# Spreading half 1's codes with TensorE and letting the loads go in steps, in a recommender tower on one core

## The reference

```python
e = jnp.stack([tbl_0[ids[:, 0]], ..., tbl_15[ids[:, 15]]], axis=1)        # 2048 x 16 x 16
A = jnp.repeat(x0, s, axis=1)                                             # x0: 2048 x 39 x 16
Bm = jnp.repeat(e, f, axis=2).reshape(b, s * f, d)
z = jnp.einsum('bnh,bnd,nk,khd,kd->bkh', A, Bm, alpha, w, hv[..., 0])      # 2048 x 16 x 16
h = jnp.concatenate([z.reshape(2048, -1), dense_ctx], axis=1)
h = jnp.maximum(h @ W_top1 + b_top1, 0.0)                                 # 272 -> 512
h = jnp.maximum(h @ W_top2 + b_top2, 0.0)                                 # 512 -> 256
y = h @ W_top3                                                            # 256 -> 1
```

## Time and profile before

| | |
|---|---|
| three runs | 177.66, 178.49 and 180.9 us, median 178.49 |
| the profiled execution | 178.92 us |
| its span, first to last instruction | 177.0 us |
| busy: PE, DVE, POOL, ACT | 164.0, 142.5, 110.9, 66.0 us |
| mean granted TensorE clock | 0.99 |

### The profile page before, as it was taken

How to read it: one execution, slowest core, us unless ns; L and a number is a source line. 1 busy time by engine, 2 the same in 40 slices (tenths; PEclk the granted TensorE clock), 3 DMA queues, 4 the chain that set the end, 5 groups by cost and what they waited for, 6 DMA issues and landing times.

```text
span 177.0 us, 5041 instructions
## 1 busy us (share of the span) xinstructions
PE 164.0 (93%) x2131; PEld 124.3 (70%) x2131; DVE 142.5 (80%) x177; ACT 66.0 (37%) x176; POOL 110.9 (63%) x116
## 2 busy tenths in 40 slices
PE   6549898968997999999999999999999999999993
PEld 1338696736984879696969696969686967776671
DVE  2978797893799999999899979996999899495000
ACT  3440788084881125212431243123403341451141
POOL 2777777777747777777777777777777776000000
PEclk9999999996999999999999999999999999999999
DMA  5889999999999997989498948694559360000000
GB/s 87 307 120 327 246 275 161 270 373 264 283 334 250 345 320 150 363 248 230 79 352 240 216 160 300 189 230 104 183 219 222 48 231 6 2 4 0 0 4 0
DMA packets 15085, 34.26 MB, mean 194 GB/s; under 512 B 6618, under 2 KB 10582, under 8 KB 11990
## 3 DMA queue, kind: packets, MB, share of 16 engines
q1 hardware_dynamic: 10162, 31.51, 58.9%
q0 software_dynamic: 3584, 0.92, 6.6%
q10 hardware_dynamic: 1316, 1.50, 2.9%
HBM read 33.88 MB, written 0.04 MB: 192 GB/s over the span
## 4 chain that ended last, share of the span: by engine, by line
PE 69%; DMA 13%; DVE 4%; ACT 3%; SPq 3%; issue 3%; POOL 3%; DVEq 0%
PE bank L927 17%; PE bank L842 17%; PE bank L848 15%; PE bank L894 11%; DMA ids_half_dram<-ids_half 6%; PE bank L915 5%; PE bank L835 4%; DMA ids_b<-ids_half_dram 3%; POOL e L478 3%; DMA e<-tbl_dram,ids_all 3%; DVE prod L642 2%; SPq L446 2%; DMA ids_all<-ids_dram 1%; ACT apart L724 1%; PE bank L856 1%
## 5 line engine op out<-in xcount | busy, mean ns | idle before, releaser
L478 POOL DMA_INDIRECT e<-tbl_dram,ids_all x112 | 110.7, 988 | 38.7 <-issue 33.2
L642 DVE TENSOR_TENSOR prod<-x,bank 128x2048 f32<-128x2048 f32 x40 | 90.3, 2279 | 8.8 <-issue 4.6
L927 PE MATMUL bank<-prod,m_w 128*32 128x256 f32 x640 | 38.6, 382 | 2.5 <-DVE prod L642 2.5
L894 PE MATMUL bank<-table,onehot 125*128 125x64 bf16 (+1 forms) x288 | 31.9, 198 | 2.3 <-DVE low L537 2.3
L842 PE MATMUL bank<-tower,w_z 128*128 128x256 f32 x128 | 32.8, 403 | 0.7 <-ACT tower L743 0.7
L894 PE MATMUL bank<-low,onehot 125*128 125x64 bf16 (+1 forms) x288 | 31.8, 197 | 0.0
L894 PE MATMUL bank<-rest,onehot 125*128 125x64 bf16 (+1 forms) x288 | 31.8, 199 | 0.0
L894 PEld LDWEIGHTS bank<-table,onehot 125*128 125x128 bf16 x288 | 27.4, 98 | 5.7 <-issue 2.9
L927 PEld LDWEIGHTS bank<-prod,m_w 128*32 128x32 f32 x640 | 19.1, 109 | 17.0 <-issue 3.5
L848 PE MATMUL bank<-tower,w 128*128 128x256 f32 x128 | 30.7, 382 | 0.1
L842 PEld LDWEIGHTS bank<-tower,w_z 128*128 128x128 f32 x128 | 24.2, 199 | 6.3 <-ACT tower L743 3.1
(11 more groups left out here) (60 smaller groups left out, 85.4 us busy)
## 6 DMA issues: line engine op xcount, KB each, us to landing
x<-x_dram SPq DMA_DIRECT2D x16, 1024.0 KB, 8.1
x<-x_dram SPq DMA_DIRECT2D x16, 512.0 KB, 12.4
ids_b<-ids_half_dram SPq DMA_DIRECT2D x7, 576.0 KB
e<-tbl_dram,ids_all POOLq DMA_INDIRECT x112, 4.7
prod<-windows_c_dram ACTq DMA_DIRECT2D x1, 768.0 KB
prod<-windows_c_dram ACTq DMA_DIRECT2D x1, 512.0 KB, 5.6
w_z<-w_z_dram SPq DMA_DIRECT2D x1, 512.0 KB
w<-w_dram SPq DMA_DIRECT2D x1, 512.0 KB, 11.0
```

Of the source, the lines that this page charges most:

```text
L478: nc.gpsimd.indirect_dma_start(out=e[:, tile, f * D:(f + 1) * D], out_offset=None, in_=t[f"tbl_{f}"][:, :], in_offset=bass.IndirectOffsetO ...
L642: nc.vector.tensor_tensor(prod[:, s % NPROD, :].rearrange("p (q b) -> p q b", q=HP), x0[:, tile % NX, :].rearrange("p (q b) -> p q b", q=H ...
L894: made = nc.tensor.matmul(o_bank[i % 2][:, at:at + m * D], onehot[:, n % 2, g, HOT.index(f), tile * P:(tile + 1) * P], parts[part][:, KT_A ...
L927: made = nc.tensor.matmul(z_bank[q * ZW:(q + 1) * ZW, a * HB:(a + 1) * HB], m_w[:, UNIT_OF[g], hp * ZW:(hp + 1) * ZW], prod[:, s % NPROD, ...
```

## The change

Five things are done.

1. Half 1's codes are spread by TensorE too (`PE_IDS = 2`): five more "ids" jobs (nine matmuls) on PE, between and after `sum_ab(0)` and `sum_ab(1)`, and five more copies on ACT. `load_ids(1)` goes away. All codes are stored by one DMA in place of seven.
2. SP lets loads go in steps. It waits until `x0` tile 1 has landed before `load_ids(2)`, for tile 2 before tile 3, for half 2's codes before the context and `w1_z`, for tile 3 before tile 4, for `w1_z` before half 3's codes, for tile 4 before `w2`.
3. Half 1's fields are regrouped (`SECOND_FILLS`): its first two fills now hold all of its fields that `spread_e(1, 0)` needs, which so waits for two fills and not for three (`kept_at`).
4. On PE at step 4, half 2's first two picks stand between half 0's last two contractions, and `turn_windows(1, 0)` right behind the last, ahead of l1. `turn_windows(0, 2)` stands ahead of fill 5.
5. On ACT `find_apart(1)` and the making of `v_dk` move forward, `spread_e(1, 0)` stands ahead of `keep_z(0)`, and `make_plane(3)` a step later. On DVE half 2's plane stands between products 2 and 3, the masks of fills 5 and 6 between products 3 and 4; `make_mask(1, 2, 8)` stands ahead of `v_diag`.

```diff
+SECOND_FILLS = [[[1, 2], [4]], [[5, 12], [15]], [[7, 10, 13]]]
-PLANE_STEPS = {1: [0, 0], 2: [4, 4], 3: [5, 6], ...
-PICK_STEPS = {1: [BEFORE, 2, 3], 2: [5, 5, 6], 3: [9, 10, 11], ...
+PLANE_STEPS = {1: [0, 0], 2: [2, 2], 3: [5, 6], ...
+PICK_STEPS = {1: [BEFORE, 2, 3], 2: [4, 4, 5], 3: [9, 10, 11], ...
-def kept_at(n, p):
-    return 2 * p + 2 if n == 0 else FIRST_FILLS[n + 1]
+def kept_at(n, j):
+    return 2 * FILL_PACK[j] + 2 if n == 0 else FIRST_FILLS[1] + 2 if (n, j) == (1, 0) else FIRST_FILLS[n + 1]
-PE_IDS = 1
-JOBS = {BEFORE: [("ids", 0, j) for j in range(0, len(HOT), 2)]}
+PE_IDS = 2
+JOBS = {BEFORE: [("ids", n, j) for n in range(PE_IDS) for j in range(0, len(HOT), 2)]}
...
-            sp.dma_start(ids_rows[1], ids_half[1:IDS:NH, :]).then_inc(ids_stored[0], 16)
+            sp.dma_start(ids_rows.rearrange("n f b -> f n b"), ids_half[:]).then_inc(ids_stored, 16)
...
-            sp.wait_ge(ids_stored[0], 16)
-            load_ids(1)
             sp.wait_ge(gathered[0][0], 16 * 2 * len(GATHERED[0][0]))
             load_x0(1)
             load_x0(2)
-            for n in range(2, NH):
-                sp.dma_start(ids_rows[n], ids_half[n:IDS:NH, :]).then_inc(ids_stored[1], 16)
+            sp.wait_ge(in_x0[1], 16 * x0_loads(1))
+            sp.wait_ge(ids_stored, 16)
+            load_ids(2)
             sp.dma_start(b_w3[:], t["b_w3"]).then_inc(in_b_w3, 16)
+            sp.wait_ge(in_x0[2], 16 * x0_loads(2))
+            load_x0(3)
+            sp.wait_ge(in_ids_b[2], 16)
             load_ctx()
             sp.dma_start(w1_z[:], t["w1_z"].rearrange("(a p) n -> p a n", p=P)).then_inc(in_w1, 16)
-            sp.wait_ge(ids_stored[1], 16 * (NH - 2))
-            load_ids(2)
-            load_x0(3)
+            sp.wait_ge(in_x0[3], 16 * x0_loads(3))
+            load_x0(4)
+            sp.wait_ge(in_w1, 16)
             load_ids(3)
+            sp.wait_ge(in_x0[4], 16 * x0_loads(4))
             sp.dma_start(w2[:], t["w2"].rearrange("(a p) n -> p a n", p=P)).then_inc(in_w2, 16)
-            load_x0(4)
...
-                for i in KEEPS.get(s, []):
+                for i in KEEPS[4] if s == 3 else KEEPS.get(s, []) if s != 4 else []:
                     mask_rows(i)
...
+            for ft in range(2):
+                keep_ab(ft)
+            find_apart(1)
             keep_rest(0)
             spread_e(0, 0)
...
                 if s == 4:
+                    spread_e(1, 0)
                     keep_z(0)
-                    spread_e(1, 0)
+                    spread_e(1, 1)
...
             sum_ab(0)
+            for job in JOBS[BEFORE][IDS_JOBS:IDS_JOBS + 2]:
+                fill_t(job)
             sum_ab(1)
+            for job in JOBS[BEFORE][IDS_JOBS + 2:]:
+                fill_t(job)
...
                     for unit in CONTRACTS[2]:
                         contract(unit)
+                    turn_windows(0, 2)
                     for i in PICKS[2]:
                         pick_rows(i)
                 if s == 4:
-                    for unit in CONTRACTS[4]:
-                        contract(unit)
+                    contract(CONTRACTS[4][0])
+                    for i in PICKS[4]:
+                        pick_rows(i)
+                    contract(CONTRACTS[4][1])
+                    turn_windows(1, 0)
                     pe.wait_ge(in_ctx, 16 * N_CTX_LOADS)
                     pe.wait_ge(in_w1, 16)
                     for job in JOBS[4]:
                         fill_t(job)
+                    turn_windows(1, 1)
```

47 lines of the change are left out of this document (21 added, 26 removed).

## The result

The changed kernel takes 177.76 us (median of 20 runs, 175.59 to 182.49) against 180.27 (20 runs, 177.66 to 185.11) for the kernel before. The ratio of the two is 0.990 [0.986, 0.994] (in brackets the 95% interval), a gain of 1.0% or about 1.8 us; the forecast was a gain of 4.6 us. The ratios here leave out executions that ran in the chip's slower state, so that they don't follow from the medians. A trace shows one execution, and the sizes read from it are those of that one.

What follows compares the result with a forecast made beforehand. PE was taken as gapless from contraction 7 on, so the time follows when DVE ends product 7. 178.92 - 3.5 (middle) - 1.6 (front clock) + 0.5 (gathers) = 174.3 us; range 173.0 to 177.2.

Steps and rivals of the forecast that it cites:

- The middle: From product 2 to product 5 on DVE, then spread and turn (1,0): 11.05 us instead of 14.55, a gain of 3.5.
- no stretch at 0.50 near 41: Sign that the forecast is right: PE's granted clock no longer at 0.50 near 41 us, around l1 of half 0.
- the front's: Up to product 2: PE's filled hole lets its clock rise with a quarter of the picks done, 1.6 us gained.
- a sign of it: Counter-evidence in the front: matmuls from 5.89 to 9.05 us and the sums behind them had not raised PE's clock.
- the clock does not rise earlier: Rival in the front: only the middle counts, 175.5 us, or 177.2 if the clock falls again near l1; chance 0.30.
- I cost this at nothing: Loads: the later issue of `w1_z`, half 3's codes, `w2` and later tiles was to cost 0 us.
- I expect them to hold nothing up: POOL's later gathers, behind half 2's first group: they gain 2.0 us from a vanished wait for a product and delay nothing.
- the 0.5: Cost in us at turn (2,0), whose spread waits for half 2's first gathers, landing at 54.0; up to 1.1 possible.
- `w1_z` landed in time: Rival at l1: `w1_z` lands late, at 46, and PE holds l1 for it: 179.2 us, or 180.9 with clock lost; chance 0.07.
- Half 2's codes were in time: Rival between products 2 and 3: DVE meets half 2's codes late; landing at 36.2 costs 3.2, giving 178.7 us; chance 0.06.
- gathers would hold ACT: Rival at turn (2,0): gathers land no sooner while the clock rises, costing 1.1 and some more: 175 to 176 us; chance 0.12.

Runs made afterwards that it cites:

- fillers: Changed kernel with nine opening matmuls of zeros instead of six and one 128x512 matmul of zeros behind each of ten spreading jobs: 177.65 us, ratio 0.991 to the kernel before.

## Why the prediction was wrong

**The middle was right.** It was to give 11.05 us from product 2 to product 5, and gave 11.27, so 3.28 and not 3.5. With turn (1,0) behind l1 again 2.47 of it is gone. That there would be no stretch at 0.50 near 41 was right too.

**The step that failed is the front's**: "I take a rise with a quarter of the picks done ... 1.6 us ... because the hole in front of the rise is what is filled." The hole was filled and the picks stayed at 64 ns, so the term is 0; product 2 gained 0.40, where the front without the clock was put at 0. The premise was that unbroken work of this kind raises the clock, and no run shows it: with nine opening matmuls, at a recorded 0.50, it did not come back from 7.7 to 17.95 us under the same spreads, sums and picks with PE busy for 4.11 of 4.30 and 3.75 of 4.00 us. The prediction had a sign of it in its own sentence, "Against it speaks that the matmuls from 5.89 to 9.05 ... did not raise the clock". The size was about right, 1.90 when fillers hold the clock. The rival "the clock does not rise earlier" is the case that came; its 175.5 is 1.3 short of the profile, mainly for the next reason.

**Two terms put at nothing were not.** "Behind its own landing wait half 3's codes, and behind tile 4 `w2` ... I cost this at nothing": the codes cost DVE 0.89 us, and products 5 to 7 took 1.0 longer for it; four kernels without this wait have contraction 7 0.7 to 1.0 sooner behind product 5. `w2` held PE for 0.65, but hidden behind DVE. And of the gathers, "I expect them to hold nothing up" behind half 2: the 0.5 was put at turn (2,0), which waited for nothing, and arose at turn (3,0), 0.6 between contraction 7 and the end. The issue moved as foreseen: the last of half 3's first gathers went out at 63.58 and not 66.06, 2.5 earlier. But it took 9.40 us to land and not 5.5, so that it landed 1.4 later, while contraction 7 came 2.7 earlier. The landing was taken as fixed; with one tile of `x0` held back it took 3.9.

The sum by what was measured: 178.92 - 3.28 - 0.40 + 1.0 + 0.6 = 176.84, the profiled 176.82. The median of the runs, 177.76, lies 0.9 above this execution, which is spread between executions, and above the range.

**The other rivals.** `w1_z` landed in time (l1 began at 41.47, right behind turn (1,0)). Half 2's codes were in time. That gathers would hold ACT was right, with another place than the one priced.

**What stays open.** That PE's stops are a late program is an inference: the traces show the count of instructions at each stop and the end of a packet 1.4 to 1.8 us before each restart, but neither what the packets hold nor when they are asked for. Whether the fillers hold the clock by their kind or by filling more of the time is open, and so is whether an order of the loads exists in which the front's 1.9 us reach the end: four orders were tried, none did it.

## What to carry to other kernels

A gain in the middle of a kernel is worth what the next resource allows, so price each of the streams behind it (loads, gathers, the last one first) against the new due time, not the old. Filling the hole on TensorE did not raise its clock here (64 ns a pick before and after): check in the trace, by the time of one matmul, at which clock the filled stretch runs before you count on it. Where the DMA engines are full (share 1.02 from 53 to 74 us here), look also for small transfers that are moved among the loads: here they were half 3's gathers (9.40 us to landing) and, if the inference holds, the 16 KB packets of queue 8, and the longest stops of PE were 2.35 us in the traces with the steps and 6.11 and 4.32 in the two without.

## What the runs showed of the hardware

- With nine opening matmuls TensorE's granted clock fell from 1.00 to 0.50 at 7.7 us, behind a stretch with PE busy for 2.16 of 3.70 us, and stayed there up to 17.95 with PE busy for 4.11 of 4.30 and 3.75 of 4.00 us. With one 128x512 matmul of zeros behind each spread as well, and 3.17 of 3.70 us busy in the first stretch, it was 1.00 from 5.56 to 36.28.
- The same gather took 9.40 us to land with the DMA engines at a share of 1.02 from 63 to 73 us (9.43 at 1.04 in a second trace), and 3.9 at 0.53, with one tile held back.
- PE stopped for up to 6.11 us in the middle of picks or of one contraction, behind 962, 1,217 or 1,474 recorded instructions (to one or two) whatever stood there, and went on 1.4 to 1.8 us behind the end of a 16 KB packet of the queue that the profile calls instruction. In none of 19 traces did PE pass such a count less than 1.37 us behind the packet that goes with it. No wait in the program names this time; the profile calls it issue.
